# A four-layer bidirectional GRU stack before a feed-forward block: the last LayerNorm is folded into the fusion, and the slot order is rewritten

## What is computed

```python
def _mingru(x, Wz, bz, Wh, bh):            # Wz = Wh = ctx[l], bz = bh = cond[l]
    z = sigmoid(einsum('bsi,hi->bsh', x, Wz) + bz)
    h_tilde = tanh(einsum('bsi,hi->bsh', x, Wh) + bh)
    a = clip(1.0 - z, CLAMP_LO, CLAMP_HI)
    return _linear_scan(a, z * h_tilde)
def _stack(x, ...):                        # 4 layers
    h = x
    for i in range(L):
        h_new = _mingru(h, ...)
        if i > 0:
            h_new = h_new + h
        h = layernorm(h_new, gamma, beta)
    return h
h_fwd = _stack(x, ...); h_bwd = flip(_stack(flip(x, axis=1), ...), axis=1)
xcond = einsum('bsi,hi->bsh', concat([h_fwd, h_bwd]), fusion_W) + fusion_b
x = x + xcond            # of layernorm(x), without gamma and beta
x = x + ffn(layernorm(x))   # ternary W_fc (512 to 2048), exact gelu, layernorm, ternary W_proj
```

## Time and profile before

| | before |
|---|---|
| median of 3 runs | 1714.82 us (1710.92 to 1716.75) |
| profiled execution | 1709.34 us, span 1707.5 us |
| TensorE matmul (PE) | busy 93% of the span |
| VectorE (DVE) | 80% |
| ScalarE (ACT) | 64% |
| GpSimd (POOL) | 64% |
| mean granted TensorE clock | 0.982 |

### The profile page before, as it was taken

One profiled execution on the slowest core, in us unless ns is written; L12 is line 12 of the kernel. 1 busy time (PEld: TensorE's weight loads), 2 busy tenths in 40 slices (PEclk: granted clock), 3 DMA queues, 4 the chain that ended last, 5 costly groups with the idle time before them and its releaser, 6 DMA issues.

```text
span 1707.5 us, 23771 instructions
## 1 busy us (share of the span) xinstructions
PE 1592.7 (93%) x8034; PEld 1313.1 (77%) x8034; DVE 1363.1 (80%) x2169; ACT 1088.6 (64%) x1789; POOL 1098.2 (64%) x1040
## 2 busy tenths in 40 slices
PE   5689998899998989999999989999999999999998
PEld 4567887777877878877778878888888788878776
DVE  6768888798988888888888874777777777777766
ACT  6478988888888888888888832343434343434344
POOL 2247876677977778977779842456565656565645
PEclk9799999999999999999999998999999999999999
DMA  4010131221130211212213361102020212111000
GB/s 154 8 49 26 37 118 55 93 93 56 31 112 26 87 50 38 86 51 82 80 31 148 109 242 33 38 29 71 27 73 32 68 33 67 35 65 36 27 19 31
DMA packets 70791, 108.77 MB, mean 64 GB/s; under 512 B 5008, under 2 KB 37776, under 8 KB 67600
## 3 DMA queue, kind: packets, MB, share of 16 engines
q1 hardware_dynamic: 66208, 99.13, 17.1%
q10 hardware_dynamic: 4464, 8.13, 1.7%
HBM read 69.50 MB, written 37.75 MB: 63 GB/s over the span
## 4 chain that ended last, share of the span: by engine, by line
PE 68%; DVE 12%; ACT 11%; POOL 5%; issue 3%; DMA 0%; ACTq 0%; DVEq 0%; SPq 0%; POOLq 0%
PE ps L387 21%; PE ps L472 13%; PE ps L490 12%; PE ps L439 10%; PE ps L421 6%; PE ps L407 4%; ACT ntok L627 2%; POOL hb L1098 2%; DVE bnp L813 2%; ACT H L649 2%; ACT hb L616 2%; DVE H L801 1%; DVE H L802 1%; ACT zb L615 1%; ACT AH L654 1%
## 5 line engine op out<-in xcount | busy, mean ns | idle before, releaser
L1098 POOL TENSOR_TENSOR hb<-zb,hb 128x512 f32<-128x512 f32 x224 | 290.0, 1294 | 155.7 <-ACT hb L616 155.5
L387 PE MATMUL ps<-AH,WH 128*128 128x512 f32 x896 | 368.9, 412 | 20.4 <-DVE H L802 8.9
L387 PE MATMUL ps<-AL,WH 128*128 128x512 f32 x896 | 352.9, 394 | 0.0
L387 PE MATMUL ps<-AH,WL 128*128 128x512 f32 x896 | 351.6, 392 | 0.0
L709 ACT ACTIVATE g<-ps 128x512 f32<-128x512 f32 x128 | 76.6, 598 | 351.2 <-PE ps L472 333.4
L1183 POOL TENSOR_TENSOR acq<-acq,sq 128x512 f32<-128x512 f32 x120 | 181.1, 1510 | 168.8 <-ACT sq L718 168.8
L795 DVE TENSOR_TENSOR_SCAN zb<-ps,hb 128x512 f32<-128x512 f32 x192 | 234.3, 1220 | 56.9 <-POOL hb L1098 54.6
L1107 POOL TENSOR_TENSOR H<-H,zb 128x512 f32<-128x512 f32 x192 | 249.6, 1300 | 0.2 <-issue 0.2
L941 DVE SCALAR_TENSOR_TENSOR gl<-g,wcol,gh 128x512 fp32r<-128x512 f32 x128 | 117.4, 917 | 146.8 <-ACT gh L715 146.8
L627 ACT ACTIVATE ntok<-ps,nbp,rsp 128x512 f32<-128x512 f32 x256 | 185.4, 780 | 54.6 <-POOL nbp L1118 54.4
L649 ACT ACTIVATE H<-ps,bet,gam 128x512 f32<-128x512 f32 x256 | 202.5, 806 | 18.5 <-PE ps L421 18.4
(11 more groups left out here) (126 smaller groups left out, 3343.0 us busy)
## 6 DMA issues: line engine op xcount, KB each, us to landing
hs_scratch<-H SPq DMA_DIRECT2D x16, 1024.0 KB, 4.8
hc<-hs_scratch SPq DMA_DIRECT2D x32, 512.0 KB, 4.2
xr<-in_x SPq DMA_DIRECT2D x32, 256.0 KB, 4.3
out<-ob SPq DMA_DIRECT2D x32, 256.0 KB, 2.2
xbuf<-in_x SPq DMA_DIRECT2D x7, 1024.0 KB, 7.3
RAW<-in_wt SPq DMA_DIRECT2D x16, 256.0 KB, 6.9
stg<-in_pjt ACTq DMA_DIRECT2D x16, 256.0 KB, 2.8
wfu_scratch<-res SPq DMA_DIRECT2D x16, 256.0 KB, 3.5
```

Source lines behind the costliest of these rows:

```text
L387: r = e.matmul(GATE[i % 3][:], w[:, q, m * 128:(m + 1) * 128], a[:, q, :], start=(n == 0), stop=(n == 11))
L1098: e.tensor_tensor(hb[c][:], zb[c][:], hb[c][:], ALU.mult).then_inc(s_p, 1)
```

## The change

For layer 3, `norm`, `back` and `feature` are gone; `tokens` and `stats` stay, and `inv` puts the inverse deviations of every token into a new tile `rl`. `H` is stored as it is after `add`. Since a direction's LayerNorm is a linear map of `H` but for the deviation of each token, the fusion is done in two halves, one for each direction, and `resid` scales each half by its `rl`. Gamma and the subtraction of the mean go into the fusion's weights: `add_rows` (PE) multiplies the raw weights by two columns (gamma over 512 and beta), the sums go through HBM and come back spread over all partitions (`put_rows`, `spread_row`), and `center` (DVE) makes gamma times weight less that row, before `high` and `rest` split them. The row of beta is added to the fusion's bias.

The slot loop now starts at slot 4; everything before is written out call by call, and the bias sums of `shift` are one group for each layer. DMAs of the absolute-value pieces are issued by SP, a slot ahead. In the slot loops the calls for new inputs and for the second tail of layer 0 have other places; for a job of layers 1 to 3 with no such neighbour the cyclic order of the calls on each engine is the same.

```diff
 ORDER = [0, 1, None] + list(range(2, NJ))
-SLOTS = range(-4, len(ORDER) + 6)
...
+            n = BANK[("W", l)]
             claim(n)
-            e.wait_ge(s_fo, KC * (L - 1))
-            for l in range(1, L):
-                for m in range(KC):
-                    r = e.matmul(RING[n % 4][:, KC * l + m:KC * l + m + 1], bw[l][:, m * 128:(m + 1) * 128], ones[:],
-                                 start=True, stop=True)
+            e.wait_ge(s_fo, KC * l)
+            for m in range(KC):
+                r = e.matmul(RING[n % 4][:, m:m + 1], bw[l][:, m * 128:(m + 1) * 128], ones[:], start=True, stop=True)
             r.then_inc(s_bp, 1)
...
+            n = BANK[("G", h)]
+            claim(n)
+            e.wait_ge(d_rw, 16 * h + 16)
+            e.wait_ge(s_gb, 2)
+            for q in range(KC):
+                r = e.matmul(RING[n % 4][0:2, :], gb[:, q, :], xbuf1[:, q, :], start=(q == 0), stop=(q == KC - 1))
+            r.then_inc(s_gp, 1)
...
-            if idx is None:
+            if idx is None or layer((what, idx)) == 3:
                 return
...
+        def fuse(u, h):
             e.wait_ge(f_sp, u + 1)
+            if u < 4:
+                claim(BANK[("F", u, h)])
+            else:
+                e.wait_ge(f_x1, 2 * u + h)
             if u == 0:
                 e.wait_ge(d_fu, 32)
-                e.wait_ge(s_sc, 4 * NJ - 2)
-            elif u == 1:
+            if u == 4 and h == 0:
                 e.wait_ge(s_sc, 4 * NJ)
-            else:
...
+            for q in range(KC * h, KC * h + KC):
                 for a, w in ((hch, FUH), (hch, FUL), (hcl, FUH)):
-                    r = e.matmul(FUSED[u][:], a[u % 2][:, q, :], w[:, q, :], start=(n == 0), stop=(n == 23))
+                    r = e.matmul(FUSED[u, h][:], a[u % 2][:, q, :], w[:, q, :], start=(n == 0), stop=(n == 11))
...
         e.wait_ge(s_c, 2)
+        back("x", 0, 1)
+        back("x", 0, 0)
+        back("x", 0, 2)
+        back("x", 0, 3)
+        mm(0, 0)
+        back("x", 1, 1)
+        back("x", 1, 0)
+        mm(0, 1)
+        back("x", 1, 2)
+        back("x", 1, 3)
+        mm(0, 2)
+        mm(0, 3)
+        mm(1, 0)
+        mm(1, 1)
+        mm(1, 2)
+        shift(1)
+        shift(2)
+        shift(3)
+        tokens(0, 0)
+        mm(1, 3)
+        tokens(1, 0)
+        tokens(0, 1)
+        back("h", 0, 2)
+        back("h", 0, 0)
+        back("h", 0, 1)
+        back("h", 0, 3)
+        tokens(2, 0)
+        tokens(1, 1)
+        tokens(3, 0)
+        tokens(2, 1)
+        mm(2, 0)
+        back("h", 1, 2)
+        back("h", 1, 1)
+        mm(2, 1)
+        back("h", 1, 3)
+        back("h", 2, 2)
+        back("h", 2, 0)
+        back("h", 2, 1)
+        mm(2, 2)
+        back("h", 1, 0)
...
-            if s == 3:
-                shift()
             if s == SUM_SLOT:
                 add_up()
-            tokens(tail_b(s - 3), 1)
-            tokens(tail(s - 2), 1)
+            if s in ROW_SLOT:
+                add_rows(ROW_SLOT.index(s))
             mm(job(s), 0)
+            back("x", batch(s + 1), 1)
+            back("x", batch(s + 1), 0)
             back("h", tail_b(s - 3), 2)
             back("h", tail_b(s - 3), 1)
             mm(job(s), 1)
             back("h", tail_b(s - 3), 3)
-            if s == 57:
-                fuse(0)
-            if s == 58:
-                fuse(1)
-                feat(0)
             back("h", tail(s - 2), 2)
+            back("x", batch(s + 1), 2)
+            back("h", tail(s - 2), 0)
+            back("h", tail(s - 2), 1)
+            back("x", batch(s + 1), 3)
+            mm(job(s), 2)
             back("h", tail_b(s - 3), 0)
-            back("h", tail(s - 2), 0)
-            back("x", batch(s + 1), 0)
-            back("x", batch(s + 1), 3)
-            back("h", tail(s - 2), 1)
-            back("x", batch(s + 1), 1)
-            mm(job(s), 2)
-            back("x", batch(s + 1), 2)
             back("h", tail(s - 2), 3)
             tokens(tail(s - 1), 0)
             mm(job(s), 3)
+            tokens(tail_b(s - 2), 1)
             tokens(tail_b(s - 1), 0)
...
-            if n + 1 < 32:
-                if n >= 1:
-                    e.wait_ge(s_abs, n)
-                e.dma_start(stg2[(n + 1) % 2][:], PIECES[n + 1]).then_inc(d_ab[(n + 1) % 2], 16)
             e.wait_ge(d_ab[n % 2], 16 * (n // 2) + 16)
             e.activation(stg2[n % 2][:], stg2[n % 2][:], ACT.Abs, accum_out=asum[:, n:n + 1]).then_inc(s_abs, 1)
...
+        def take_rows(h):
+            e.wait_ge(s_gv, h + 1)
+            if h == 0:
+                e.wait_ge(s_bp, L - 1)
+            dst = (raw0[0:2, :], xbuf1[0:2, 0, :])[h]
+            e.activation(dst, RING[BANK[("G", h)] % 4][0:2, :], ACT.Copy).then_inc(s_gr, 1)
...
+            if idx is None or layer((what, idx)) == 3:
+                return
             u = (what, idx, m)
-            if idx is None or layer(u) == 3:
-                return
             s = 2 * (idx % 2) if what == "x" else place(TAILS[idx])
             e.wait_ge(s_ah, HIGHS[u])
             e.tensor_tensor(AL[s][:, m, :], RING[BANK[u] % 4][:], AH[s][:, m, :].bitcast(F32), ALU.subtract).then_inc(s_al, 1)
...
+        def bias_rows(h):
+            e.wait_ge(s_gp, h + 1)
+            if h == 0:
+                e.wait_ge(d_fb, 16)
+            else:
+                e.wait_ge(s_gv, 1)
+            e.tensor_tensor(fbb[0:2, :], RING[BANK[("G", h)] % 4][0:2, :], fbb[0:2, :], ALU.add).then_inc(s_gv, 1)
+        def center(n):
+            e.wait_ge(d_raw[n % 2], 16 * (n // 2) + 16)
+            e.wait_ge(d_fb, 32 if n < 4 else 48)
+            e.scalar_tensor_tensor(raw[n % 2][:], raw[n % 2][:], gam[:, n % KC:n % KC + 1], fbb[:], ALU.mult,
+                                   ALU.subtract).then_inc(s_ct, 1)
...
+        def resid(u, h):
+            b, t, i, r = u // 4, u % 4, u % NX1, u % 2
+            e.wait_ge(f_fu, 2 * u + h + 1)
...
+                    e.wait_ge(d_res[2], 16 * 16)
+                if u >= NX1:
+                    e.wait_ge(f_fin, u - NX1 + 1)
+                e.scalar_tensor_tensor(x1[i][:], FUSED[u, 0][:], rl[:, b, 0, t:t + 1], xr[u % 3][:], ALU.mult,
+                                       ALU.add).then_inc(f_x1, 1)
+                return
+            e.wait_ge(f_x1, 2 * u + 1)
+            e.scalar_tensor_tensor(x1[i][:], FUSED[u, 1][:], rl[:, b, 1, t:t + 1], x1[i][:], ALU.mult,
+                                   ALU.add).then_inc(f_x1, 1)
+            e.wait_ge(f_x1, 2 * u + 2)
             e.bn_stats(bn[:, r, 0, :], x1[i][:]).then_inc(f_b1, 1)
             e.wait_ge(f_b1, u + 1)
             e.bn_aggr(mv[:, r, 0, :], bn[:, r, 0, :]).then_inc(f_a1, 1)
...
+        input_stats(0)
+        input_stats(1)
+        low_weights(0, 2)
+        low_weights(0, 3)
+        low("x", 0, 0)
+        low("x", 0, 1)
+        low("x", 0, 2)
+        low("x", 0, 3)
+        fold(1)
+        keep(0, 0)
+        low("x", 1, 0)
+        low("x", 1, 1)
+        scan(0, 0)
+        keep(0, 1)
+        low("x", 1, 2)
+        scan(0, 1)
+        low("x", 1, 3)
+        keep(0, 2)
+        scan(0, 2)
+        keep(0, 3)
+        scan(0, 3)
+        keep(1, 0)
+        fold(2)
+        low_weights(1, 0)
+        low_weights(1, 1)
+        low_weights(1, 2)
+        low_weights(1, 3)
+        scan(1, 0)
+        keep(1, 1)
+        scan(1, 1)
+        fold(3)
+        biases(1)
+        biases(2)
+        biases(3)
+        stats(0, 0)
+        keep(1, 2)
+        stats(1, 0)
+        scan(1, 2)
+        stats(0, 1)
+        keep(1, 3)
+        scan(1, 3)
+        low("h", 0, 2)
+        low("h", 0, 0)
+        low("h", 0, 1)
+        low("h", 0, 3)
+        stats(2, 0)
+        stats(1, 1)
+        stats(3, 0)
+        low_weights(2, 0)
+        low_weights(2, 1)
+        low_weights(2, 2)
+        low_weights(2, 3)
+        low_weights(3, 0)
+        low_weights(3, 1)
+        low_weights(3, 2)
+        low_weights(3, 3)
...
             scan(job(s - 2), 2)
             stats(tail(s - 3), 1)
             keep(job(s - 2), 3)
-            scan(job(s - 2), 3)
+            input_stats(batch(s + 2))
+            if s == 57:
+                cut(0)
             if s == 58:
                 cut(1)
-            if s == 57:
-                cut(0)
-            input_stats(batch(s + 1))
-            if s == 0:
-                fold(1)
-            if s == 0:
-                for k in (2, 3):
-                    e.wait_ge(s_wh, k + 1)
-                    e.tensor_tensor(WL[0][:, k, :], RAW[0][:, k, :], WH[0][:, k, :].bitcast(F32), ALU.subtract).then_inc(s_wd, 1)
-            if s == 1:
-                fold(2)
-            if s == 2:
-                fold(3)
+            aside(s)
+            scan(job(s - 2), 3)
             keep(job(s - 1), 0)
+            low("x", batch(s), 0)
+            if s == 5:
+                bias_rows(0)
+            if s == 22:
+                thresholds()
+            low("h", tail_b(s - 4), 2)
+            low("x", batch(s), 1)
```

(43 more changed lines are left out.)

472 lines of the change are left out of this document (301 added, 171 removed), and 3 rows, old and new, of the table START_RING.

## The result

The changed kernel takes 1686.17 us, median of four runs (1685.17 to 1686.63), against 1712.87 (1710.30 to 1716.75) for the kernel before: a ratio of 0.9841, 95% interval [0.9819, 0.9864]. The forecast was 1693.3. The executions of one kernel can differ by a few us, as the four of before do, so what an edit did is read first from marks inside the profiled executions, and whole times come second.

What follows compares the result with a forecast made beforehand. PE was taken to bound regular slots and the feed-forward stage, ACT and DVE also counting after layer-0 jobs. Terms -21 -5 -7 +5 +3 +2.5 +1 = -21.5 us gave median 1693.3; own range 1680 to 1704, whole range 1667 to 1713.

Steps and rivals of the forecast that it cites:

- Part 1: Layer 3's way back in the stack: removing norm, transposes back and H writes gains 21 us, between 12 and 27.
- Part 3: Order in slots after layer 0, with piece loads moved to SP: -7 us, between +6 and -25.
- DMA issues 1: Absolute-value piece loads leaving ACT's queue, 0.33 us per issue, nearly all in slots PE sets: 1 us gained.
- Order 6: Slots after layer 0: moved input statistics, normalisation and transposes, and second tail's transposes, gain 6 us.
- Part 2: The start: first matmul 3 us earlier, job 2 some 5 us early; net -5 us, between +3 and -14.
- they now run while job 1 still has matmuls: The start: bias sums, formerly together in 5.3 us behind a 3.9 us PE wait, now run during job 1's matmuls.
- Part 4: Folding gamma, beta and mean into fusion weights: add_rows on PE +5 us (3.6 to 7.6), center on DVE +3 (0 to 12).
- Rival C: DVE's queue in the stack: center waits for late pieces and delays scans, giving 1724 us; chance 0.07.
- Part 5: Fusion in two halves, feed-forward stage: 28 more group starts of 0.09 us, +2.5 us, up to +8.
- Part 6: Turn from stack to feed-forward stage: transposes go but DVE's chain sets the pace; +1 us, between -3 and +4.
- Rivals A and B: Slots after layer 0: A, new order fills them, middle 1670, chance 0.20; B, removed transposes were cover, middle 1706, chance 0.10.
- Rival D: Slots behind layer 3 keep their 14.7 us because ACT or DVE has an equal period: 1714 us; chance 0.06.

Runs made afterwards that it cites:

- e1: Kernel before with only layer 3's norm, transposes back and feature removed, last LayerNorm's scaling, gamma and beta left out: 1688.98 us, ratio 0.9867.
- e5: Changed kernel with 16 unread identity transposes put back on PE two slots behind each layer-3 job: 1704.35 us, ratio 0.9947.
- e11: Changed kernel with loads of the absolute-value pieces issued by ACT again, one piece ahead, instead of by SP: 1697.24 us, ratio 0.991.
- e2: Changed kernel without add_rows, bias rows, center and their loads (gamma, beta and mean left out): 1674.01 us, ratio 0.9773.
- e9: Changed kernel with both add_rows sets in the start and the first LayerNorm ahead of layer 1's low parts and fold(3): 1669.14 us, ratio 0.9747.
- e12: e9 with the last pair's token transposes between first and second fusion, their statistics right behind the first residual: 1666.59 us, ratio 0.9735.

## Why the prediction was right, and where it was not

The time was 7 us below the forecast, inside its range, for a sum whose parts were off by more than that in both directions; that they cancelled is luck. (Of the 7 us, 2 are the median of before, 1714.82 when the sum was made and 1712.87 with a fourth run.)

- **Part 1**, -21 between -12 and -27: 21.9 in the old order (e1), 17.7 of PE alone in the new one (e5). The regular slot behind layer 3 came to 12.66 us, forecast 12.8, in four of the five places; the fifth, job 55's, kept its 14.1 us with new idle time of PE, which my last paragraph had called a sign of being wrong. Three of the four are helped by the order, which moved 2 us of DVE into the slot ahead: with part 1 alone they stayed at 13.3 us (e1). That ACT's relief is in this sum is argued from the difference of the two, not shown by itself.
- **Part 3**, -7, between +6 and -25: the failed term. The order is worth 14.9 to 19.1 us in jobs 10 to 55 alone. Both of its terms were too small. "DMA issues 1" rests on the step "each issue took ACT's queue 0.33 us, nearly all of it in slots that PE sets": by e11 these loads cost up to 12.6 us, 5.4 of them in jobs 10 to 55, because ACT waits for them. In the profile of before the rows were there, ACT's waits for `stg`, and I had read the issue's length instead of them. "Order 6" had no working of its own, and 8.6 us came from job 20 on alone; which moved call brought them stays open. PE's two waits for `ntok` fell from 30.3 to 25.7 us, below 30 as said, and by less than the gain, so they were not its measure.
- **Part 2**, -5 net: job 0 came 3.5 us earlier, as forecast (-3), but job 2 came 5.2 later, not 5 earlier. e2, without fold work, starts job 10 2.4 us before the kernel before. That can't be told from the scatter of the start; and the moved loads, worth up to 7.1 us ahead of job 10 by e11, are in it too, so that without them the new start may well be a loss. The step that failed is "they now run while job 1 still has matmuls". I counted the sums' 5.3 us and not what stands behind them: PE waits 13 us for two folds, with the first LayerNorm's transposes queued behind. The eight low parts took 5.4 us, one every 673 ns, less than my 7.7: the 957 ns are a mean of nine of 0.74 us and three of 1.3 to 1.8, and I took the mean for each. The same holds for `center`, 745 ns. e9 shows that the gain was to be had: with both sets of `add_rows` in its start, job 2 begins at 83.6, 1.6 us ahead of before, and job 10 7.3 ahead.
- **Part 4**, +8 in all: +10.4 for `add_rows` (forecast 5) and +0.5 for `center` (forecast 3), by e2. The upper price per set was right (3.59 of 3.8 us). What failed is that the first set would fall in idle time: after's stretch from 90.45 has 3.4 us of it left instead of 11, and the set cost 3.0 of its 3.6 us; the second cost 6.6, with new idle time of PE around it.
- **Rival C** needed `center` to wait for its piece, 4.4 us each. No DVE wait names L1054. Nor was it lengthened: 743 to 749 ns, where I had worked out up to 1.5 us, and +8 instead of +3, from the rule of the Trainium skill (SBUF — State Buffer, "Who interferes with whom"). The trace shows the rule's effect elsewhere (below). At the start of all eight `center` a POOL instruction was under way, but it ended within 0.3 us, and the next one, where there was one, began after `center` had begun; so these rows are no test of a long one.
- **Part 5**, +2.5: in its steady part a batch of four units takes 85.6 us from its first `g` to the next one's, before 85.0, so the five batches of that part cost 3 us, near the forecast. The size is right, the reason in part: once a batch PE waits 0.6 us for `n` (3.8 us in six waits behind the turn), where before it waited for `hcl` (2.3 us in seven). That difference, 0.3 us a batch, goes with the later norm and is about half of what the batch lost; only the rest can be the groups' starts, which the forecast had. The first batch is 2.0 us shorter than before's (93.8 against 95.8), and the stage as a whole the same, 687.6. The half costs DVE 739 ns and nobody waits for it; PE was busy for 98.1% of the stage, as said.
- **Part 6**, +1 between -3 and +4: +5.8, outside its bounds, as `add_rows` was with 10.4 against 3.6 to 7.6. I looked at DVE's chain and not at banks: the last pair's transposes want the bank of the second unit's residual (4.6 us), and the third fusion wants theirs (2.6 us). e12 takes 3.9 us of it back by order alone.
- **Rivals A and B**: A's premise, that the disturbed slots fill, held for one class. Slots like job 29's have 0.3 us of PE idle left; those like job 32's stayed at 19.5 to 19.8, with DVE at 19.3. B's premise, cover, holds for a quarter of the transposes in the new order (e5). Rival D fell with the 12.66 us slot.

## What to carry to other kernels

A load that an engine issues for itself shortly before its use costs that engine the wait, not the issue: look for the engine's wait on the DMA, and let an idle queue issue it a stage ahead. When sums or folds are put into a start, ask for each queue what chain stands behind them; the first consumer of the next stage goes first, and preparation fills its gaps (here 15 us, e9 against after in the stack's end, of which 8 came with `add_rows`). When a stage ends on a ring of banks, follow who claims whose bank before pricing the instructions.

## What the hardware showed

- The same DVE instruction has two durations. `x<-c,sg,x` in after (min/median/max ns):

```profile
L1183 DVE SCALAR_TENSOR_TENSOR x<-c,sg,x x32: 736/1249/1784, 1117.8 to 1678.9; 128x512 f32<-128x512 f32 x32
```

  Sixteen last about 0.74 us, with POOL busy beside them for 4% of the time, sixteen about 1.78, with a POOL instruction already running at the start of each, in twelve of them the addition of the next unit (L1425). That is the rule of the Trainium skill named above, and the trace agrees. `n<-x,mv,rs`, with a single large SBUF operand but of a form (`tensor_scalar`) that the same section lets use the shared pair, takes 1.48 to 1.52 us beside POOL in 28 cases and 0.54 in the four where POOL is idle. The two residuals, which read one operand from PSUM, take 736 to 751 ns, the ones that lie beside a POOL instruction too.
- A plain f32 matmul of 512 columns is two instructions of 449 ns, start to start; an fp32r one takes 228.
- After the stop of 9.0 us PE restarts at the lower of its two clocks: eight transposes took 1.95 us at 61.32, with a granted clock of 0.50 (1.2 GHz of 2.4), and 1.03 at 67.09, with 1.00. In the turn, with 12.3 us of idle time instead of 5.8, the mean granted clock was 0.85 instead of 0.96. So a stop of PE costs more than its own length.
